# The transposes of the next group's maxima in slot 0 of a group, in place of slot 1

## The reference, cut to what matters

```python
q, k, v = split_heads(x @ Wq), split_heads(x @ Wk), split_heads(x @ Wv)
attn = softmax(einsum('bhqd,bhkd->bhqk', q, k) * e ** -0.5, axis=-1)
attn = attn + bias[None]            # from rel_table, by position
out = einsum('bhqk,bhkd->bhqd', attn, v)
out = (out - mu) / sqrt(var + 1e-3) * gamma + beta
```

## Time and profile before

| | us |
|---|---|
| median of 3 runs | 2076.93 (2070.39 to 2079.27) |
| the profiled execution | 2077.11 |
| its span | 2075.4 |
| loop over the groups in it | 920.2 to about 1343 |

### The profile page before, as it was taken

One profiled execution on the slowest core, in us unless ns is written; L12 is line 12 of the kernel. 1 busy time (PEld: TensorE's weight loads), 2 busy tenths in 40 slices (PEclk: granted clock), 3 DMA queues, 4 the chain that ended last, 5 costly groups with the idle time before them and its releaser, 6 DMA issues. The chain is left out here.

```text
span 2075.4 us, 33422 instructions
## 1 busy us (share of the span) xinstructions
PE 1697.8 (82%) x9958; PEld 1155.9 (56%) x9959; DVE 1203.9 (58%) x1926; ACT 1086.7 (52%) x2285; POOL 614.9 (30%) x560
## 2 busy tenths in 40 slices
PE   4988898482299969899999999942599999999990
PEld 1333333282199836443444444441499999999990
DVE  6999998386611155357999999258433333333334
ACT  5777776440033324127788888612355555555554
POOL 0000000000156422211222222100377777777760
PEclk9999999755599979988999999855699999999995
DMA  3000001354022096603333333066244444444427
GB/s 127 1 0 0 0 0 41 102 185 162 9 67 64 29 308 226 132 3 71 76 96 96 96 96 91 22 219 232 72 66 73 69 68 69 68 67 69 70 22 243
DMA packets 150376, 182.07 MB, mean 88 GB/s; under 512 B 29683, under 2 KB 110974, under 8 KB 150144
## 3 DMA queue, kind: packets, MB, share of 16 engines
q1 hardware_dynamic: 108512, 136.68, 21.6%
q0 software_dynamic: 33536, 43.71, 12.3%
q10 hardware_dynamic: 8224, 0.39, 0.2%
HBM read 115.96 MB, written 70.65 MB: 90 GB/s over the span
## 5 line engine op out<-in xcount | busy, mean ns | idle before, releaser
L1284 PEld LDWEIGHTS f_ht_ps<-f_XT,f_WS 128*128 128x128 f32 x2944 | 359.9, 194 | 15.9 <-DVE f_WS L1377 2.7
L1284 PE MATMUL f_ht_ps<-f_XT,f_WS 128*128 128x128 f32 x2944 | 363.4, 277 | 3.2 <-ACT f_XT L1325 1.4
L1292 PE MATMUL f_y_ps<-W,f_HT 128*128 x1472 | 347.9, 379 | 0.0
L2099 DVE TENSOR_REDUCE att_MX<-att_s_ps 128x2 f32<-128x1024 f32 x256 | 305.8, 1217 | 68.3 <-PE att_s_ps L1856 68.1
L1248 POOL DMA_INDIRECT moe<-f_Y,TOK x184 | 278.3, 1512 | 183.1 <-ACT f_Y L1350 145.6
L2062 ACT ACTIVATE att_PT<-att_st_ps 128x512 f32<-128x512 f32 x512 | 278.8, 595 | 77.5 <-PE att_st_ps L1881 69.7
L1292 PEld LDWEIGHTS f_y_ps<-W,f_HT 128*128 128x128 f32 x1472 | 265.5, 190 | 28.6
L1377 DVE COPY f_WS<-W 128x1024 f32 x184 | 135.0, 735 | 212.0 <-issue 109.1
L303 PE MATMUL rec_gate<-rec_XC,rec_W 128*128 128x512 f32 x384 | 188.7, 645 | 68.9 <-ACT rec_R L205 42.8
L1881 PE MATMUL att_st_ps<-att_Q,att_K 50*128 50x512 f32 x512 | 223.1, 491 | 19.4 <-ACT att_PT L2062 19.0
L1385 DVE TENSOR_TENSOR f_Y<-f_y_ps,f_B 128x256 f32<-128x256 f32 x144 | 61.2, 425 | 296.4 <-PE f_y_ps L1292 296.4
(11 more groups left out here) (262 smaller groups left out, 2280.8 us busy)
## 6 DMA issues: line engine op xcount, KB each, us to landing
W<-in_w SPq DMA_DIRECT2D x48, 512.0 KB, 10.0
att_Q<-qk_pairs SPq DMA_DIRECT2D x192, 64.0 KB, 2.9
att_K<-qk_pairs SPq DMA_DIRECT2D x192, 64.0 KB, 3.0
qk_pairs<-prj_HI SPq DMA_DIRECT2D x16, 512.0 KB, 3.8
qk_pairs<-prj_LO SPq DMA_DIRECT2D x16, 512.0 KB, 5.1
rec_H<-in_xT SPq DMA_DIRECT2D x8, 512.0 KB, 7.8
recurrent_T<-rec_H SPq DMA_DIRECT2D x8, 512.0 KB, 3.3
n_YT<-recurrent_T SPq DMA_DIRECT2D x8, 512.0 KB, 3.9
```

The source lines that it names most:

```text
L1284: mm = nc.tensor.matmul(ht_ps[r % 2][:, f * P:(f + 1) * P], WS[r % 2][:, at:at + P], XT[r % 2][:, c], start=(c == 0), stop=(c == DC - 1))
L1292: mm = nc.tensor.matmul(y_ps[r % 2][:], HT[r % 2][:, f], W2[:, bass.ds(e * W_EXPERT + f * D, D)], start=(f == 0), stop=(f == FC - 1))
L2099: nc.vector.tensor_reduce(MX[n % 2][:, qc, :, p], s_ps[m % 2][:], AX.X, ALU.max).then_inc(s_mx, 1)
```

## The change

`maxima(n + 1)` is called at the end of a group's slot 0 and no longer at the end of its slot 1. It is the same call with the same waits, for all n from 0 to 30. In slot 1 it stood behind one piece of `sums`; slot 0 has no such piece. The lists of ACT, DVE, POOL and SP are as before.

```diff
@@ -1970,7 +1970,7 @@
                         sums(n - 1, at - 1)
                     if at == PIECES - 1 and n >= 1:
                         sums(n - 1, at)
-                    if p == 0 and slot == 1 and n + 1 < NGROUPS:
+                    if p == 0 and slot == 0 and n + 1 < NGROUPS:
                         maxima(n + 1)
                     if p == 0 and slot == 3 and n >= 2:
                         sums_T(n - 2)
```

## The result

| | before | changed |
|---|---|---|
| median of 6 | 2076.68 us (2070.39 to 2079.27) | 2090.23 us (2088.29 to 2091.59) |
| the profiled execution | 2077.11 | 2090.14 |
| its span | 2075.4 | 2088.4 |
| mean granted clock of it | 0.883 | 0.876 |

Ratio 1.0067, 95% interval 1.0052 to 1.0082: the change costs 13.6 us, 0.67%. That is more than the 0.5% that a measurement tells from no change, so the case "slower" came, which had a chance of 0.40; the time forecast, 2086, is 4 us short of it, and the range held it. One execution in all that follows, one of the kernel "C alone moved" (2123.56 us), lies over 1.5% above the fastest of its kernel and is left out of its median and ratio.

The account below looks back on a forecast made before the run. No engine is full over the span; the attention loop is a PE-ACT ping-pong, one late in each slot. Terms -4.65 + 6.0 + 1.3 (+2.7), plus 6.4 for clock falls, gave +9.1: 2086 us, range 2068 to 2098.

Parts of the forecast that it names:

- the case "slower": Whole kernel measured above the 2087.3 us bound of what can be told from no change; chance 0.40.
- A: Attention-loop groups 10, 14, ..., 26 (12.40 us, 2.6 us of ACT idle): gain of 0.37 us each.
- B: Attention-loop groups 7, 11, ..., 27 (12.90 us, filled by ACT): no change, bounds 0 and -0.35 us each.
- C: Attention-loop groups 8, 12, ..., 28 (12.99 us, filled by DVE): PE waits for the late split, costing 1.0 us each.
- D: Attention-loop groups 9, 13, ..., 29 (12.66 us, filled by ACT): slot 1 starts later, costing 0.22 us each.
- the forecast's own upper branch: Stall in C with three clock falls: +12.3 us; the forecast with one to three falls had chance 0.48.
- Gains, 4.65 us: Attention loop: 0.44 us in each of groups 2 to 6, 0.37 in five A's, 0.6 for groups 0, 1, 30.
- The falls, two of 3.2 us: TensorE's clock drops to half after two of the six C's, at 3.2 us each: +6.4 us.
- The ends of the loop: Groups 0, 1 and 30 together: gain of 0.6 us, between 0 and 1.2.
- Rival 3: In C the split's cast starts before POOL's add, the split ends within 1 us, C gains: 2066.5 us; chance 0.13.
- Rival 1: No clock fall after C's stall: +2.7 us, 2079.7 us, or 2082 with the gains halved; chance 0.20.
- Rival 2: Clock falls after four to six C's, 3.2 to 3.9 us each: 2092 to 2103 us; chance 0.19.

Follow-up runs that it names:

- C alone moved: Kernel before, with the transposes moved to slot 0 in groups 8, 12, ..., 28 alone: 2093.86 us (median of five), ratio 1.0109.
- POOL's new order and slot 1: Kernel before (transposes in slot 1), with POOL's residual put ahead of the add of a group's output: 2072.13 us, ratio 0.9985.
- the filled kernels: Changed kernel with three, or two, unused 128x512 products on PE ahead of C's wait for the split: 2077.99 us (1.0010), or 2079.31 us (1.0016).
- second profile: The changed kernel measured once more, unchanged: 2087.44 us in two runs, ratio 1.0055.
- the pause on POOL: Changed kernel with three 128x1 memsets on POOL between the residual's multiply and its add: 2083.62 us, ratio 1.0042.
- POOL's residual first: Changed kernel (slot 0) with POOL's residual put ahead of the add of a group's output: 2065.00 us, ratio 0.9947.

## Why the prediction was right, and where it was off

*The mechanism held*: gains in A and groups 2 to 6, nothing in B, a stall in C with falls of the clock behind some of them, a little in D. The case that came is the forecast's own upper branch, three falls, which had been put at +12.3; the profiles differ by 13.0. That these agree so well is partly luck. By the table, the groups 2 to 29, which the mechanism speaks of, give +8.4, of which 7.5 are the falls, where the forecast had +12.9 for them (-4.05 + 6.0 + 1.3 + 9.6). The rest, +4.6, comes from groups 0, 1 and 30 and from outside the loop, where the forecast had a gain of 0.6.

*Gains, 4.65 us.* A was put at 0.37 us, with DVE late at the end, and groups 2 to 6 at 0.44. Both measured 0.51 to 0.52 (3 to 6 and A). DVE didn't limit A, and slot 2's exponentials in group 14 start 0.51 us earlier (3.47 us in, where it was 3.98). Together they gave 4.9 us in this profile and not 4.05, so this term was 0.8 us too small.

*C, 1.0 us each.* Measured 0.75 to 0.9 at full clock. The steps stood as forecast: wait 2.19 us, slot 1 at 3.46 (3.48 forecast), slot 3's first product at 6.12 (6.19).

*D, 0.22.* Measured 0.13 to 0.16.

*The falls, two of 3.2 us.* This is the term that was mis-sized on both sides. There were three in the first profile and four in the second, at 1.0 to 3.7 us, most often 2.4 to 2.5 for 6.8 us at half clock. The price per us was 0.35 and not 0.29. The 0.29 came of a wrong comparison: group 1 at a mean clock of 0.60 (16.10 us) was set against A at full clock (12.40), but group 1 has less to do: the copy of the sums and their transposes begin with group 2. Against itself it gives the right price: in the kernel with POOL's new order and slot 1 it took 14.57 us at a mean clock of 0.70, so 1.53 us less for 4.1 us less at half clock, 0.37 us per us (by which it would take about 11.3 us at full clock, an estimate). The length was wrong too, 12.9 us at the loop's start, but 3.4 to 10.2 in a C. The falls are 7.5 us of the first profile and, by the filled kernels, 8 to 12 us of the median.

*The ends of the loop* were put at a gain of 0.6 between groups 0, 1 and 30; the profile has +3.9. Most of it can't be put down to the change: group 1 took 16.10 us before and 18.14 after, but 14.49, 18.14 and 13.64 in three experiments whose PE lists up to there are the changed kernel's, and 14.42 in its second profile. How long the clock stays low there (13.7 to 30.7 us, from 917 to 923 on) differs from execution to execution. Group 30 moves likewise, 18.0 to 21.2 us. A difference of 4 us there, between two single profiles, shows nothing of the change.

*Rival 3* failed in its working, not only in its chance. It said that a cast which goes first ends the split within 1 us. Twice in the changed kernel's first profile (groups 12 and 28), and in all C's with the pause on POOL, the cast did go first, and the subtraction behind it was held for 2.2 us. The gain it named (2066.5) is real, but takes both instructions out of POOL's way: 2065.0.

*Rival 1* (no fall) is what the filled kernels come near: forecast 2079.7, measured 2078.0 and 2079.3. They aren't the changed kernel, though: three products add 0.4 us to each C, and the gains and C's stall were each smaller or larger than forecast. *Rival 2* had its condition, four falls, met in the second profile of the changed kernel, and its price was too high: that execution took 2087.54 us and not 2092, since the four falls cost 10.8 us (1.0, 3.7, 2.4 and 3.7) and not 12.8, and its groups 0 and 1 were 3.3 us shorter than before.

## What to carry to other kernels

A late producer may cost little behind one slot (0.55 us here) and nearly its whole length behind the one before it (2.0 of 2.2): before moving a consumer earlier, read when its producer ends in every kind of iteration, not in the common one, for here six of 31 calls decided the sign. When one engine's short instruction shows ten times its usual length, look at what runs beside it before moving anything around it, since taking that collision away was worth 3.9 us with the transposes in slot 1, and some 25 with them in slot 0, where the best that the move gave without it was 4.9 (slot 0 in A and groups 2 to 6 alone). And price an idle stretch of PE with what the clock may do afterwards: here 2.2 us of idle time cost 0.9 us by itself and up to 3.7 more by the clock.

## What the runs showed of the hardware that was not expected

A stretch of 2.0 to 2.2 us without an instruction on PE, 2.6 to 2.7 up to the first product that is no transpose, was followed by a fall in seven of twelve C's of the two profiles of the same kernel, and in 11 of 24 with the two other kernels that have this stretch. After a stretch of 2.2 us it was 9 of 14, after one of 2.03 to 2.10 us 2 of 10, too few to tell the two apart. The low clock then lasted 3.4, 6.8 or 10.2 us. All eleven began 2.2 to 4.8 us into the group. The three that began within PE's idle stretch (2.2 to 2.6 us in) lasted 10.2 us, the eight that began after slot 1's products had started lasted 3.4 or 6.8. Products that nothing uses, covering the stretch but for 0.3 us or wholly, left none (twelve C's in two profiles). One fall (group 7 of the kernel with POOL's residual first) came without such a stretch and was not explained.

Two VectorE instructions of 0.18 us can each be held for 2.2 us by the same GpSimd instruction, and which of them it is turns on 0.02 us. It changes little in when the second one ends (2.87 or 2.72 us into the group), and a C at full clock took 13.88 us with the one and 13.75 with the other. The held instruction shows as running all that time, with no idle time and no releaser, so its duration is the only sign.
